# Embedding gathers at an even pace: due times by share of the block instead of steps between two turns

## The reference

```python
e = jnp.stack([tbl_f[ids[:, f]] for f in range(40)], axis=1)            # 2048 x 40 x 32
iidx, jidx = jnp.triu_indices(40, k=1)                                  # 780 pairs
z = jnp.einsum('bpd,pde,bpe->bp', e[:, iidx], bilinear_matrices, e[:, jidx])
h = jnp.concatenate([z, dense_ctx], axis=1)                             # 796 wide
h = jnp.maximum(h @ W_top1 + b_top1, 0.0)                               # 512
h = jnp.maximum(h @ W_top2 + b_top2, 0.0)                               # 256
y = h @ W_top3                                                          # 1
```

## Time and profile before

| | before |
|---|---|
| median of 3 runs | 984.23 us |
| the profiled execution | 994.04 us, span 992.1 us |
| TensorE busy, mean granted clock | 840.1 us (85%), 0.881 |
| VectorE, ScalarE, GpSimd busy | 585.6 us, 199.3 us, 418.3 us |
| gathers | 430, mean 971 ns |
| bytes moved | 22.68 MB, mean 23 GB/s |

### The profile page before, as it was taken

The page is one execution under the profiler, slowest core; times in us unless marked ns, Lnnn a source line. Parts: engine busy times, 40 slices in busy tenths (PEclk is TensorE's granted clock), DMA queues, the critical chain, the costliest instruction groups (busy, mean ns, idle before and its releaser), DMA issues.

```text
span 992.1 us, 18558 instructions
## 1 busy us (share of the span) xinstructions
PE 840.1 (85%) x8058; PEld 321.9 (32%) x8058; DVE 585.6 (59%) x701; ACT 199.3 (20%) x362; POOL 418.3 (42%) x437
## 2 busy tenths in 40 slices
PE   3215588877688999899989998997999999799999
PEld 2002244333232333232223232332332323345445
DVE  3002447654235888895348686881686879447551
ACT  4002123111121220221202212211323122131122
POOL 7773645566545345544554364436321332300000
PEclk8555777887777999998789999997999999899999
DMA  4103912200020101010101001000100000000000
GB/s 96 16 13 65 123 46 68 53 12 11 10 33 10 23 10 31 11 24 10 32 11 24 7 11 31 10 19 12 21 13 4 10 14 13 8 2 2 1 3 1
DMA packets 62571, 22.68 MB, mean 23 GB/s; under 512 B 45283, under 2 KB 61677, under 8 KB 62490
## 3 DMA queue, kind: packets, MB, share of 16 engines
q1 hardware_dynamic: 48702, 14.37, 6.9%
q0 software_dynamic: 13760, 7.07, 5.5%
q10 hardware_dynamic: 28, 0.06, 0.0%
HBM read 21.40 MB, written 0.07 MB: 22 GB/s over the span
## 4 chain that ended last, share of the span: by engine, by line
PE 73%; issue 12%; another core or an unknown queue 8%; DVE 3%; ACT 3%; DMA 0%; DVEq 0%; ACTq 0%
PE U L825 21%; PE bank_z L850 19%; PE misc L880 12%; PE misc L771 11%; PE U L834 5%; DVE prod L722 2%; PE U L880 1%; PE U L798 1%; PE U L794 1%; PE bank_z L858 1%; ACT x_twin L559 1%; ACT x_T L541 1%; DVE ones L686 0%; ACT x_twin L562 0%
## 5 line engine op out<-in xcount | busy, mean ns | idle before, releaser
L490 POOL DMA_INDIRECT rows<-in_tbl,idx x430 | 417.5, 971 | 443.6 <-PE U L794 126.7
L722 DVE TENSOR_TENSOR prod<-U,x_T 128x1024 f32<-128x1024 f32 (+1 forms) x314 | 343.5, 1129 | 105.3 <-PE U L825 72.4
L850 PE MATMUL bank_z<-prod,select 128*32 128x512 f32 (+1 forms) x2000 | 241.2, 548 | 10.0 <-issue 9.6
L825 PE MATMUL U<-x_T,W 32*128 32x512 f32 (+1 forms) x1440 | 207.5, 563 | 34.0 <-issue 15.9
L771 PE MATMUL misc<-ones,tabs 125*32 125x512 bf16 (+1 forms) x1890 | 144.6, 374 | 57.1 <-issue 56.0
L686 DVE TENSOR_SCALAR ones<-idx_wide,row_of 125x2048 bf16<-125x2048 f16 (+3 forms) x180 | 107.5, 625 | 111.3 <-remote 83.2
L722 DVE TENSOR_TENSOR prod<-U,x_look 128x1024 f32<-128x1024 f32 (+1 forms) x90 | 88.8, 1006 | 96.8 <-PE U L825 52.3
L825 PEld LDWEIGHTS U<-x_T,W 32*128 32x128 f32 x1440 | 82.2, 192 | 130.7 <-issue 64.1
L771 PEld LDWEIGHTS misc<-ones,tabs 125*32 125x32 bf16 x1890 | 71.2, 104 | 148.4 <-issue 116.9
L880 PE MATMUL misc<-z,W 128*32 128x512 f32 (+1 forms) x952 | 108.8, 549 | 0.8 <-ACT x_look L541 0.6
L850 PEld LDWEIGHTS bank_z<-prod,select 128*32 128x32 f32 x2000 | 49.5, 112 | 168.5 <-issue 128.4
(11 more groups left out here) (71 smaller groups left out, 307.2 us busy)
## 6 DMA issues: line engine op xcount, KB each, us to landing
rows<-in_tbl,idx POOLq DMA_INDIRECT x430
idx_wide<-idx_rows SPq DMA_DIRECT2D x6, 500.0 KB
idx_wide<-idx_rows SPq DMA_DIRECT2D x6, 375.0 KB
idx_wide<-idx_rows SPq DMA_DIRECT2D x3, 187.5 KB
W<-in_W_top SPq DMA_DIRECT2D x35, 2.0 KB
W<-_L_rec_bilinear_matrices SPq DMA_DIRECT2D x4, 128.0 KB
W<-in_W_top SPq DMA_DIRECT2D x1, 512.0 KB
idx_wide<-idx_rows SPq DMA_DIRECT2D x2, 250.0 KB
```

What stands on the lines that cost most here:

```text
L490: nc.gpsimd.indirect_dma_start(out=rows[:, n % R_SLOTS, t, f, :], out_offset=None, in_=tables[field][:, :], in_offset=bass.IndirectOffsetO ...
L722: last = nc.vector.tensor_tensor(to[:, :, m * N:(m + n) * N].rearrange("p r (m n) -> p r m n", m=n), U[:, at:at + 2, m * N:(m + n) * N].re ...
L825: last = nc.tensor.matmul(U[:, at + r % 2, m * N:(m + 1) * N], W[row, at_W:at_W + P], x_of(o, a)[row, :], start=True, stop=True, skip_grou ...
L850: last = nc.tensor.matmul(bank_z[r * DIM:(r + 1) * DIM, 0:N], sel, prod[:, (2 * g + r // 2) % P_SLOTS, r % 2, m * N:(m + 1) * N], start=(k ...
```

## The change

The steps between two turns are dropped. Every gathered field of every block gets a due time of its own: the fields of a block, in the order of the turns, are spread evenly over the block's cycles, and the whole sequence is moved 0.8 of a block ahead of TensorE (LEAD). A field whose due time would be before cycle 0 does not wait. The wait for the slot (`turned`) stays, and the first field of a slot now waits for its due time too.

```diff
-TURN_CYCLE = [g for g in range(-2, G) for _ in TURN_AT[g]]
+LEAD = 0.8
+GATHER_ORDER = [[(c, f) for oo, c in TURNS if oo == o for f in GATHERED[(o, c)]] for o in range(BLOCKS)]
+
+
+def due(o, c, f):
+    at = o + GATHER_ORDER[o].index((c, f)) / len(GATHER_ORDER[o]) - LEAD
+    b = int(at)
+    return int(FIRST_CYCLE[b] + (at - b) * (FIRST_CYCLE[b + 1] - FIRST_CYCLE[b])) if at > 0 else 0
+
+
+DUE = {(o, c, f): due(o, c, f) for o in range(BLOCKS) for c, f in GATHER_ORDER[o]}
+assert all(at + 6 <= g or at == 0 for (o, c, f), at in DUE.items() for g in TURN_AT if (o, c) in TURN_AT[g])
...
             for n, (o, c) in enumerate(TURNS):
                 if n >= R_SLOTS:
                     pool.wait_ge(turned, n - R_SLOTS + 1)
-                for i, f in enumerate(GATHERED[(o, c)]):
+                for f in GATHERED[(o, c)]:
                     field = CF * CHUNK_OF_STEP[c] + f
-                    if n >= R_SLOTS and i:
-
-                        freed, next_freed = TURN_CYCLE[n - R_SLOTS], TURN_CYCLE[n - R_SLOTS + 1]
-                        if freed + i * (next_freed - freed) // len(GATHERED[(o, c)]) > 0:
-                            pool.wait_ge(summed, freed + i * (next_freed - freed) // len(GATHERED[(o, c)]))
+                    if DUE[(o, c, f)]:
+                        pool.wait_ge(summed, DUE[(o, c, f)])
```

## The result

The changed kernel takes **908.46 us** (median of four runs, 903.66 to 911.60) against 984.07 (981.98 to 992.34) for the kernel before in the same comparison: a ratio of 0.921, with a 95% interval from 0.914 to 0.928. Repeated later with both kernels unchanged, it gave 910.27 against 983.6 (0.925, 0.920 to 0.929). On two other chips the kernel before takes 764 us, and on the one of them on which the change was timed it does nothing; that belongs to the explanation and comes with the experiments.

A forecast was written before the change was run, and what follows sets the result against it. Runs of more than four gathers without a pause were taken to nearly stop TensorE, busy 85% of the span. Gains of 73.7 us less 22 us of costs gave 51.7 us, so 932 us; range 907 to 968.

The forecast's parts named there:

- The signs named beforehand: After 100 us no run over eight gathers; full clock at block ends; less "issue" idle; cycles 75 to 80 near 22 us.
- the prediction's own bounds of the terms: Extremes of the summed terms: 910 us with free runs of 8 and all gains, 967 us at the other end.
- the four new runs of 8: Dues one cycle apart at 35/36, 60/61, 85/86 and 110/111 each make eight gathers in a row: 5.5 us each, 22 us cost.
- the old pair: Two runs of 8 gathers in block 2, beside six cycles taking 32.8 us against 21.7 undisturbed: 11.1 us gain.
- the stretch at cycles 0 to 2: Stretch at 118.3 us: 13 records in 7.0 us should take 1.4, a gain of 5.6 us.
- the block ends, 13.5 each: Runs of 16 gathers with their aftermath: 15 us each, 1.5 remaining for the twin copy; gains 13.5, 13.5 and 13 us.
- 857.5: Stretch at 857.5 us: 103 records in 17.8 us should take 11.0 or less, being half as wide; 7 us gain.
- cycles 2 to 22: Block 0, with dues at every cycle as before: nothing changes, since GpSimd rests 1.21 us between fields; 0 us.
- More than four without a pause: TensorE nearly stops from about the fifth gather of a run without a pause until shortly after the last.
- Rival D: More gain: block 0 speeds up too with its higher clock, giving 900 us; chance 0.04.
- Rival B: Slower: block 0's fields join into one run, 20 fields costing 110 us, giving 1037 us; chance 0.06.
- Rival A: No effect: stalls sit at block ends and gathers only coincide, or each gather costs the same anywhere; 984 us, chance 0.10.

The follow-up runs named there:

- e2: Kernel before, due times untouched, with a rest of three waited memsets (some 2 us) after every fourth gather past the 56th: 881.73 us, ratio 0.899.
- e1: Changed kernel with only the first field of a slot waiting for its due time, the others following at once: 1139.97 us, ratio 1.159.
- e4: Changed kernel with the due times of blocks 2 and 3 at least two cycles apart: 903.93 us, ratio 0.921.
- the two pairs: Traces of the kernel before and the changed kernel, both unchanged, in the first comparison and its repetition: gains of 90 and 73.6 us.
- e8b: Kernel before with one waited memset (some 0.8 us) after every fourth gather past the 56th: 965.16 us, ratio 0.979.
- e3: Changed kernel with a rest of some 2 us after every fourth of the first 56 gathers only: 897.92 us, ratio 0.916.
- the first two sets: Comparisons on two chips where the stall is present; the kernel before takes 981.82 us in one and 983.6 us in the other.
- a3: Changed kernel, unchanged, run again on a chip without the stall: 763.79 us, ratio 1.001 to the kernel before.
- f2: Kernel before with six waited memsets (some 4 us) after every eighth gather past the 56th, on a chip without the stall: 820.98 us, ratio 1.075.

## Which step of the prediction failed, and what held

**The bound and the direction: right where the stall is.** e2 moves nothing but the spacing and turns 982 into 882; e1 keeps each slot's first due time and gives up the spacing, and turns 908 into 1140. The stalls of the earlier trace rows were the gathers' and not the block ends'. The signs named beforehand are there: runs of at most eight, full clock at both ends, 21.6 us for cycles 75 to 81. The sign of a falling "issue" share came by luck, as the second execution shows (10%).

**The size: gain forecast 51.7, measured 75.6 by the medians.** The measured 908.46 lies beyond the 910 that the prediction's own bounds of the terms give at best; its range began at 907 without a term for the rest. The step that failed is the cost of the four new runs of 8, 22 us. It took half of the old pair's 11.1 us for each. The windows at 468.8 and 559.2 pass 83 and 72 records in 10 us at full clock, against 94 undisturbed; e4 puts a run at 2.5 us, and cycles 31 to 73 with 81 to 123 lost 7.1 and 8.9 us in the two pairs. This is 12 to 15 us of the miss. The old pair was two runs 12 us apart with a fallen clock (0.90), and that half of it is not the price of a single run is the likely reason; no run parts the two. Second, the stretch at cycles 0 to 2 was costed from the seven microseconds of the earlier trace rows alone, 5.6 us; the two whole cycles gained 16.1 and 11.3. Third, the block ends, 13.5 each: 1.5 us was to remain for the twin copy "whatever the gathers do", but that wait is gone (427.72 above), and 86 records at 9.4 per us were to take 9.2 and take 6.8; 73 to 75 and 123 to 125 gained 17.6 to 22.3. At 857.5 the narrower records were discounted too far (7; 11.1 to 11.5). Against these, cycles 2 to 22 were put at nothing and lost 5.5 and 10.8.

**Right in its size:** 75 to 81 (11.1 forecast, 11.2 and 8.3), 25 to 31 (10; 9.8 and 7.8), and in the first pair 22 to 25 (13; 13.4, then 9.1). The start stayed but for 4.6 and 2.7 us.

**Misread in the prediction, without weight in the sum:** turn 43 makes a run of ten gathers, not of 16, since a field of block 4 has two. Block 4's last fields come due at every cycle (175 to 178), not at every second. In slice 11 GpSimd has 5 tenths between 6 and 4, so it does not stand out there as it does at slice 28.

**The criterion was too narrow.** "More than four without a pause" came from runs whose pauses were 2.87 us. Rests of 1.21 us were taken as harmless in block 0; but with rests of 2 us cycles 12 to 22 take 38.4 us (e2) against 58.8 before and 65.2 after, so the two kernels lose some 20 and 27 us there. That the short rests are the cause is in part argued: 22 gathers stand beside these ten cycles in e2, and 34 and 42 in the other two. e8b confirms it with 0.82 us. Rival D's gain was there to be had, and the change does not take it. Rival B's mechanism (block 0 closing up) shows in part: cycles 2 to 22 lose 5.5 us in the first pair and 10.8 in the second, and e3 shows its full price, 40 us for 34 gathers without a rest.

**Rival A, and the rule behind it.** In the first two sets the trace does not agree with the Trainium skill, page SBUF — State Buffer, section Who interferes with whom, by which TensorE waits on nobody: 15 records in 38 us beside 31 gathers. In a3 the trace agrees: 356 beside the same 31, a run of 350 gathers without effect, and rival A's outcome of no effect (763.79 against 763.90). Rival A thus depends on a condition that no trace of before shows. The forecast gave it 0.10 on another ground (that gathers and stalls only coincide); whether the gathers do harm at all is a property of the chip, or of its state then, and not of the kernel.

**Open:** whether the chip itself or its condition at the time makes the difference, as no chip was met in both conditions, and what in it; by which way gathers stop TensorE, as neither their transfers' timing nor GpSimd's busy time differs; and whether the gathers in a row or the mean pace (1.38 us each stalls, 1.7 does not) decides.

## What to carry to other kernels

When TensorE issues a matmul every 1.4 us behind idle time that nothing explains, look at what GpSimd issues beside it: sixteen to twenty small indirect gathers 1.25 us apart cost 18 to 22 us here, and rests of 2 us after every four removed that. Give the gathers a pace in time rather than a count of cycles: a cycle is shorter where the engine is well fed, and late due times close up into the very run that they should prevent. Measure on more than one chip before paying for it: where there is no stall, the even pace is free, but the inserted rests cost 1 to 11%.

## What the runs showed of the hardware

- The kernel before takes 982 to 984 us on two chips and 764 on two others, each within 1%, so 22% less on the second two. GpSimd is busy for 419.9 and 426.6 us with the same gathers in the traces of after and a3. What differs is TensorE: idle for 117.5 against 32.8 us and, at a mean clock of 0.936 against 0.984, busy for 784.4 against 728.6.
- Under the stall a gather's packets still start 1.65 us after issue. What stands is TensorE, in the start at 0.4 records per us in steps of 0.70 us, and its clock is at 1.2 GHz (0.50) there.
- The price of a run grows faster than its length: 2.5 us for 8 gathers and some 7 for 10 (both by e4), 18 to 22 for 16 to 20 (cycles 73 to 75 and 123 to 125).
- The best version under the stall is e2 at 882 us, the kernel before with rests; none beats 764 on the other chips. The even pace (908 and 764) is the better of the two where the chip is not known, if no version may lose on either: e2's rests were not timed on a chip without the stall, and the same mean rest every eight gathers (f2) cost 7.5% there.
